# Second product of the first feed-forward in rounded high and low parts, with the square sums and first rows inside the last attention units

## The reference

```python
# layer 0
a = attention0(layernorm(x))        # 16 query heads, 4 key heads, head width 128, window 64 + first 32 keys
gu = ln @ ternary(w_gate_up).T      # 2048 columns: gate, up
h = silu(gate) * up                 # 1024 columns
hn = h / sqrt(mean(h * h) + eps)
f = hn @ ternary(w_proj).T          # 256 columns: the product this change touches
x = x + a_out * silu(f)             # a_out = attention output times wo0
# layer 1: the same frame, plain attention with 16 heads of width 16, feed-forward with gelu
x = x + a1_out * silu(gelu(ln @ W0.T + b0) @ W1.T + b1)
```

## Time and profile before

| | us |
|---|---|
| median of 3 runs | 816.56 (815.56 to 816.63) |
| the profiled execution's own time | 815.04 |
| its span | 813.2 |
| PE busy | 770.1 |
| DVE busy | 607.1 |
| ACT busy | 474.0 |
| POOL busy | 299.8 |

### The profile page before, as it was taken

The page is one execution under the profiler, slowest core; times in us unless marked ns, Lnnn a source line. Parts: engine busy times, 40 slices in busy tenths (PEclk is TensorE's granted clock), DMA queues, the critical chain, the costliest instruction groups (busy, mean ns, idle before and its releaser), DMA issues.

```text
span 813.2 us, 13362 instructions
## 1 busy us (share of the span) xinstructions
PE 770.1 (95%) x4656; PEld 475.5 (58%) x4656; DVE 607.1 (75%) x1632; ACT 474.0 (58%) x968; POOL 299.8 (37%) x255
## 2 busy tenths in 40 slices
PE   4977899899999999999999999999999999999996
PEld 2555578555356667846446667856436667865543
DVE  6979887679766766788857677887958677787852
ACT  3888872535867773243777675143795765233583
POOL 1358770401028882002008885002005887100201
PEclk9989999999999999999999999999999999999998
DMA  9311012381013110084003120047002200027300
GB/s 302 105 46 46 1 32 81 123 224 44 3 33 87 59 33 1 1 253 112 2 13 101 33 65 2 1 156 208 3 2 52 80 21 1 1 77 216 73 3 26
DMA packets 56818, 55.37 MB, mean 68 GB/s; under 512 B 14256, under 2 KB 43312, under 8 KB 56752
## 3 DMA queue, kind: packets, MB, share of 16 engines
q1 hardware_dynamic: 52768, 49.63, 21.5%
q10 hardware_dynamic: 3664, 3.84, 1.7%
q0 software_dynamic: 320, 1.05, 0.4%
HBM read 39.00 MB, written 15.24 MB: 67 GB/s over the span
## 4 chain that ended last, share of the span: by engine, by line
PE 68%; issue 12%; DVE 8%; ACT 5%; POOL 5%; DMA 1%; ACTq 0%; SPq 0%; POOLq 0%; DVEq 0%
PE bank L931 13%; PE bank L1042 7%; PE bank L1249 6%; PE bank L1233 5%; PE bank L966 5%; PE bank L1144 5%; PE bank L1028 5%; PE bank L1172 4%; PE bank L1216 3%; PE bank L1009 3%; PE bank L977 2%; PE bank L1221 2%; POOL region L598 2%; PE bank L991 2%; POOL region L602 2%
## 5 line engine op out<-in xcount | busy, mean ns | idle before, releaser
L1605 DVE TENSOR_REDUCE mx<-bank 128x1 f32<-128x512 f32 x256 | 161.2, 684 | 28.2 <-PE bank L1172 23.1
L602 POOL TENSOR_TENSOR region<-region 128x512 f32<-128x512 f32 x75 | 100.3, 1337 | 148.0 <-DVE region L1423 143.3
L931 PE MATMUL bank<-xnT,wrope 128*128 128x512 f32 x320 | 147.4, 604 | 5.2 <-DVE th L1446 2.1
L883 ACT ACTIVATE region<-bank 128x512 f32<-128x512 f32 x256 | 132.9, 602 | 25.5 <-PE bank L1221 24.2
L762 ACT ACTIVATE region<-region,nb 128x128 f32<-128x128 f32 x256 | 81.5, 390 | 57.1 <-DVE nb L1435 56.8
L931 PEld LDWEIGHTS bank<-xnT,wrope 128*128 128x128 f32 x320 | 58.9, 194 | 67.5 <-issue 62.9
L598 POOL TENSOR_TENSOR region<-region,sin_sb 128x512 f32<-128x512 f32 x60 | 81.5, 1358 | 40.7 <-ACT region L742 40.1
L631 POOL TENSOR_TENSOR region<-region,bo_bc 128x256 f32<-128x256 f32 x16 | 11.6, 727 | 204.6 <-DVE region L1484 204.6
L1416 DVE TENSOR_TENSOR region<-bank,cos_sb 128x512 f32<-128x512 f32 x80 | 54.3, 686 | 34.5 <-PE bank L931 34.2
L740 ACT ACTIVATE region<-bank 64x512 f32<-64x512 f32 x80 | 47.5, 594 | 48.7 <-DVE region L1416 39.2
L966 PE MATMUL bank<-region 128*128 128x128 f32 x512 | 73.1, 287 | 1.0 <-POOL region L602 1.0
(11 more groups left out here) (143 smaller groups left out, 1344.8 us busy)
## 6 DMA issues: line engine op xcount, KB each, us to landing
wrope<-in_wrope SPq DMA_DIRECT2D x80, 128.0 KB, 2.2
scratch<-region SPq DMA_DIRECT2D x16, 512.0 KB, 5.0
Qp<-scratch SPq DMA_DIRECT2D x56, 128.0 KB, 3.6
Kp<-scratch SPq DMA_DIRECT2D x56, 128.0 KB, 3.7
scratch<-region SPq DMA_DIRECT2D x16, 256.0 KB, 5.4
X<-in_x SPq DMA_DIRECT2D x4, 512.0 KB, 4.1
out<-X SPq DMA_DIRECT2D x16, 128.0 KB, 2.1
VW<-v_rows SPq DMA_DIRECT2D x16, 102.0 KB, 2.7
```

Source lines behind the costliest of these rows:

```text
L602: nc.gpsimd.tensor_tensor(dst, dst, tiles(sw[:, r % 2, :], i), ALU.add)\
L883: nc.scalar.activation(P1[:, n % 8, :], turned_bank(n)[:, :], ACT.Exp, scale=SCALE1)\
L931: mm = nc.tensor.matmul(misc(b, name)[:, 0:width], lhs(c), xnT[:, c, :], start=(c == 0), stop=(c == DC - 1))
L1605: nc.vector.tensor_reduce(mx1[:, g % 2, column:column + 1], scores_bank(m)[:, :], AX.X, ALU.max)\
```

## The change

The second product takes its weights from two rounded copies of `H` (`H_hi` and `H_lo`, which lie in the buffers `Qp` and `Kp`), and `wpT` is stored rounded as well. ACT writes `H_hi` (`high_rows`), DVE writes `H_lo = H - H_hi` (`low_rows1`). Each 8-chunk product of a tile becomes 16 products of rounded values. The sums of squares stand in unit 16 with a bank of their own, tile 0 behind them, tile 1 in unit 17. The root is scaled by one half (`4.0 / HID`), the tanh reads the product's bank with the root as its scale, the gate reads the bank too, and the residual is added with the root as its factor, so that L1539 is gone. `rsqrt` has 11 links. `FFN_LATER` is another list, and the raw pieces of the weights that lay in `wpT` lie in `H`.

```diff
-RSQRT = 13
+RSQRT = 11
@@ misc_jobs
-    jobs += [("proj", 0), ("proj", 1), ("ot", 1), ("wo0", 0), ("wo0", 1), ("proj", 2), ("proj", 3)]
-    jobs += [("xh", 0), ("wo0", 2), ("wo0", 3), ("xh", 1), ("v1", 0)] + ...
+    jobs += [("sum", 0), ("proj", 0), ("proj", 1), ("proj", 2), ("ot", 1), ("wo0", 0), ("wo0", 1), ("proj", 3)]
+    jobs += [("wo0", 2), ("wo0", 3), ("xh", 0), ("xh", 1), ("v1", 0)] + ...
-FFN_LATER = [0, 0, 2, 2, 0, 0, 2, 2, 0, 0, 2, 2, 2, 1, 1, 0]
+FFN_LATER = [0, 1, 1, 2, 0, 1, 2, 2, 0, 1, 2, 2, 1, 1, 0, 0]
+def ups_at(b, s):
+    return [i for kind, i in ffn_at(b, s) if kind == "up"] if 0 <= s < NKV * TT else []
-        wpT = sb("wpT", [P, HC, DIM])
+        wpT = sb("wpT", [P, HC, DIM], F32R)
+        H_hi, H_lo = Qp, Kp
-        wp_flat = wpT[:, :, :].rearrange("p c n -> p (c n)")
+        h_room = [h_flat[:, n * SEQ:n * SEQ + PIECE] for n in (HC - 3, HC - 5)]
@@ scalar
+            def high_rows(b, i):
+                act.wait_ge(h_ready.sem, h_ready.at(b, i + 1))
+                nc.scalar.activation(H_hi[:, i, :], H[:, i, :], ACT.Copy).then_inc(hhi_ready.sem, 1)
+                    for i in ups_at(b, s - 1):
+                        high_rows(b, i)
-                turned_outputs(b, 1)
                 for t in range(TT):
-                    act.wait_ge(f_ready.sem, f_ready.at(b, t + 1))
-                    nc.scalar.activation(TE0[:, t, :], F[:, t, :], ACT.Tanh, scale=0.5)\
+                    if t == 2:
+                        turned_outputs(b, 1)
+                    misc_wait(act, b, ("proj", t))
+                    if t == 0:
+                        act.wait_ge(fr_step.sem, fr_step.at(b, RSQRT))
+                    nc.scalar.activation(TE0[:, t, :], misc(b, ("proj", t))[:, 0:DIM], ACT.Tanh, scale=rstd[:, t:t + 1])\
@@ tensor
-                        mm = nc.tensor.matmul(misc(b, ("proj", t))[:, 0:DIM], H[:, c, t * P:(t + 1) * P],
-                                              wpT[:, c, :], start=(c == 0), stop=(c == HC - 1))
+                        if t == 0:
+                            pe.wait_ge(hlo_ready.sem, hlo_ready.at(b, c + 1))
+                        for part in (H_hi, H_lo):
+                            mm = nc.tensor.matmul(misc(b, ("proj", t))[:, 0:DIM], part[:, c, t * P:(t + 1) * P],
+                                                  wpT[:, c, :], start=(c == 0 and part is H_hi),
+                                                  stop=(c == HC - 1 and part is H_lo))
+                def square_sums():
+                    pe.wait_ge(sq_ready.sem, sq_ready.at(b, 1))
+                    misc_take(pe, b, ("sum", 0))
+                    pe.wait_ge(mx0_done.sem, mx0_done.at(b, NT * (NKV * TT - 1)))
+                    ...
                     if s == NKV * TT:
-                        pe.wait_ge(h_ready.sem, h_ready.at(b, HC))
-                        projected(0)
+                        square_sums()
+                    if s >= NKV * TT:
+                        misc_done(projected(s - NKV * TT), ("proj", s - NKV * TT))
-                misc_done(projected(1), ("proj", 1))
-                turn_outputs0(b, 1)
-                projected(2, 0, 2)
+                misc_done(projected(2), ("proj", 2))
+                turn_outputs0(b, 1)
+                projected(3, 0, HC // 2)
                 pe.wait_ge(ot_ready.sem, ot_ready.at(b, 2))
                 output0(0)
                 output0(1)
-                misc_done(projected(2, 2), ("proj", 2))
-                misc_done(projected(3), ("proj", 3))
-                turn_half(b, 0)
+                misc_done(projected(3, HC // 2), ("proj", 3))
                 output0(2)
                 output0(3)
+                turn_half(b, 0)
@@ vector
+            def gate0(b, t):
+                misc_wait(dve, b, ("proj", t))
+                gate_of(b, 0, t, misc(b, ("proj", t))[:, 0:DIM])
+            def low_rows1(b, i):
+                dve.wait_ge(hhi_ready.sem, hhi_ready.at(b, i + 1))
+                nc.vector.tensor_tensor(H_lo[:, i, :], H[:, i, :], H_hi[:, i, :], ALU.subtract)\
+                    .then_inc(hlo_ready.sem, 1)
+                    for i in ups_at(b, s - 2) if s >= NKV * TT else ():
+                        low_rows1(b, i)
+                    if s == NKV * TT:
+                        misc_wait(dve, b, ("sum", 0))
+                        rsqrt(misc(b, ("sum", 0))[:, 0:TT], 4.0 / HID, 16 * EPS_RMS, fr_step, b, 0)
                     ... (first_blocks, ternary steps, gate and times_up)
+                    for i in ups_at(b, s - 2) if s < NKV * TT else ():
+                        low_rows1(b, i)
+                    if s == NKV * TT + 1:
+                        gate0(b, 0)
-                    for t in pair:
-                        gated_ffn(t)
-                    for t in pair:
-                        gate_of(b, 0, t, F[:, t, :])
-                    for t in pair:
-                        gated_attention(t)
+                    if h == 0:
+                        gate0(b, 1)
+                        for t in pair:
+                            gated_attention(t)
+                        for t in pair:
+                            row_stats(b, 1, t)
+                    else:
+                        for t in pair:
+                            gate0(b, t)
+                            gated_attention(t)
+                            row_stats(b, 1, t)
```

More of the change, by code:

```diff
@@ L71, in misc_jobs @@
         jobs += [("wt", k) for k in TURN_AT.get(s, ())] if b == 0 else []
-    jobs += [("proj", 0), ("proj", 1), ("ot", 1), ("wo0", 0), ("wo0", 1), ("proj", 2), ("proj", 3)]
-    jobs += [("xh", 0), ("wo0", 2), ("wo0", 3), ("xh", 1), ("v1", 0)] + [("qk", j) for j in range(4)] + [("v1", 1)]
+    jobs += [("sum", 0), ("proj", 0), ("proj", 1), ("proj", 2), ("ot", 1), ("wo0", 0), ("wo0", 1), ("proj", 3)]
+    jobs += [("wo0", 2), ("wo0", 3), ("xh", 0), ("xh", 1), ("v1", 0)] + [("qk", j) for j in range(4)] + [("v1", 1)]
     jobs += [("dup", i) for i in range(HC)] + [("mt", 0)] + [("down", t) for t in range(TT)]
@@ L87, in misc_order @@
     return order
-PLACED = {"xt": (2, 6), "xh": (3, 0), "qk": (1, 2, 3, 4), "v1": (5, 7), "dup": (2, 2, 2, 2, 3, 4, 2, 3), "down": (4, 1, 2, 3), "mt": (2, 2, 3, 2)}
-LENT = {("rope", 1): 3, ("rope", 2): 4, ("wo1", 1): 3, ("wo1", 2): 4, ("wo1", 3): 5, ("proj", 2): 4, ("proj", 3): 5, ("wo0", 2): 0, ("wo0", 3): 6}
+PLACED = {"xt": (2, 6), "sum": (5,), "xh": (3, 0), "qk": (1, 2, 3, 4), "v1": (5, 7), "dup": (2, 2, 2, 2, 3, 4, 2, 3), "down": (4, 1, 2, 3), "mt": (2, 2, 3, 2)}
+LENT = {("rope", 1): 3, ("rope", 2): 4, ("wo1", 1): 3, ("wo1", 2): 4, ("wo1", 3): 5, ("proj", 2): 4, ("proj", 3): 5, ("wo0", 0): 3, ("wo0", 1): 6, ("wo0", 2): 0, ("wo0", 3): 6}
 def misc_banks(order):
@@ L402, in released @@
                 "up": lambda: [(h_ready, n + 1)],
-                "proj": lambda: [(f_ready, n + 1)],
+                "proj": lambda: [(g_ready, n + 1)],
+                "sum": lambda: [(fr_step, 2)],
                 "wo0": lambda: [(sg_step, n + 1)],
@@ L1041, in projected @@
                     for c in range(first, last):
-                        mm = nc.tensor.matmul(misc(b, ("proj", t))[:, 0:DIM], H[:, c, t * P:(t + 1) * P],
-                                              wpT[:, c, :], start=(c == 0), stop=(c == HC - 1))
-                    return mm
+                        if t == 0:
[4 more added lines that the diff above has]
+                                                  stop=(c == HC - 1 and part is H_lo))
+                    return mm
+                def square_sums():
+                    pe.wait_ge(sq_ready.sem, sq_ready.at(b, 1))
+                    misc_take(pe, b, ("sum", 0))
+                    pe.wait_ge(mx0_done.sem, mx0_done.at(b, NT * (NKV * TT - 1)))
+                    for n in range(TT):
+                        mm = nc.tensor.matmul(misc(b, ("sum", 0))[:, n:n + 1], sq[:, 1, n * P:(n + 1) * P],
+                                              ones1[:, :], start=True, stop=True)
+                    misc_done(mm, ("sum", 0))
                 for s in range(NKV * TT + 2):
                     if s == NKV * TT:
-                        pe.wait_ge(h_ready.sem, h_ready.at(b, HC))
-                        projected(0)
+                        square_sums()
+                    if s >= NKV * TT:
+                        misc_done(projected(s - NKV * TT), ("proj", s - NKV * TT))
                     if s < NKV * TT:
@@ L1067, in _ @@
                         turn_weights(k // 2, k % 2)
[L1070 to L1074, removed]
                 def output0(t):
@@ L1365, in rsqrt @@
                     lambda: nc.vector.scalar_tensor_tensor(out=y, in0=a, scalar=1.5, in1=y,
+                                                           op0=ALU.add, op1=ALU.mult),
+                    lambda: nc.vector.tensor_tensor(a, y, y, ALU.mult),
+                    lambda: nc.vector.tensor_tensor(a, a, h, ALU.mult),
+                    lambda: nc.vector.tensor_scalar(v, a, 1.5, 2.5, ALU.mult, ALU.add),
```

(14 more changed lines are left out.)

20 lines of the change are left out of this document (6 added, 14 removed).

## The result

The changed kernel takes **832.25 us** (median of 5 runs, 827.48 to 833.91); the kernel before took 816.22 beside it (5 runs, 815.28 to 816.63). The ratio is 1.0192 (95% interval 1.0159 to 1.0225): slower by 16.0 us. The forecast was 820.6, range 810 to 830: the direction was right, the loss was four times the one forecast (4.1), and the time lies above the range. The profiled execution took 827.48 us (span 825.6, mean granted clock 0.977). It is the shortest of the five; the other four took 831.53 to 833.91 at 0.970 to 0.975. The profiled execution of before took 815.04 (span 813.2, clock 0.989). So the two traces show 12.4 us of the loss, and the rest lies in executions without a trace.

The account below looks back on a forecast made before the run. PE was taken to bound units and tail of batches 1 to 3, with DVE counting in batch 0. First norm -0.4, batch 0 +5.7, batches 1 to 3 -1.2: +4.1 on 815.04, 819.1; median 1.5 above, 820.6 us, range 810 to 830.

Parts of the forecast that it names:

- PE's price: Second product on PE: a rounded 256-column product takes 0.13 us, a tile 2.08 for 3.56, 23.7 us less in all.
- Rival 3: Second product on PE: the rounded product is no faster, at 0.235 us each; +27.6, 844 us; chance 0.05.
- What is added: Per batch, eight copies on ACT at some 0.6 us and eight subtractions on DVE at 0.7 or 1.1 us.
- Rival 2: DVE and POOL block each other: at 1.5 us a subtraction, +11.6, 828 us; chance 0.12.
- Tail of batches 1 to 3: Sums at 316.4, then DVE is the path: `turn_half(1)` at 339.95 for 340.37; three batches -1.2 us.
- expected second gap: Tail of batch 1: PE, ready at 338.7, waits for DVE's normalised rows ahead of `turn_half(1)` at 339.95.
- Batch 0: Seven subtractions cost +5.0 in the units, PE waits for POOL's squares, the tail is 0.7 late: +5.7 us.
- Units of batches 1 to 3: DVE's subtractions make PE reach unit 16 at 316.4 instead of 313.8 in batch 1, 2.6 us late; bounds 0 and 4.
- Rival 1: Units of batches 1 to 3: subtractions fall into DVE's idle time and PE's gain survives; 809.7 us; chance 0.26.
- Rival 4: The terms cancel: units late by 1.5 instead of 2.6 us in three batches, -3.3, 817.3 us; chance 0.15.

Follow-up runs that it names:

- warm: The changed kernel with needless products on PE in its long waits, which nobody reads; 826.19 us, ratio 1.0124 to the kernel before.
- no_low: The changed kernel without DVE's subtractions, the product taking H_hi twice, so the low part is missing; 818.13 us, ratio 1.0032 to the kernel before.
- rsqrt11_before: The kernel before with 11 links in the root chain instead of 13, nothing else; 813.07 us, ratio 0.9973.
- few_squares_before: The kernel before, with POOL squaring only the last of the eight parts of H; 816.13 us, ratio 1.0006.

## Why the prediction was right in direction and wrong in size

**PE's price: right.** Timeline of PE in tile 0 of batch 1, the kernel after: products 0.12 us apart (forecast 0.13).

```profile
326.95 0.28 PE L1062 MATMUL bank<-wpT,Kp 128*128 128x256 f32 x1
327.07 0.28 PE L1062 MATMUL bank<-wpT,Qp 128*128 128x256 f32 x1
```

The rule of the Trainium skill that was weighed ("TensorE: Matmul & The Clock Gate", section "The mechanism": loads overlap only where row groups differ) fails here again: these products have a load of 0.20 us each (its group's mean is 197 ns) and start every 0.12. The same section also lets a load run ahead when it goes to a background weight buffer; the pace agrees with that, though no run here shows where a load goes. Rival 3 is dead. Tiles take 2.0 to 2.1 us at full clock, four a batch, so some 23.7 us were taken off PE's products. PE is busy only 10 us less, and most of the difference is the clock: layer 1's q and k products alone are busy 42.2 us for 33.2 (in warm 33.6).

**What is added: right.** Groups of the kernel after, busy us and mean ns of one:

```profile
L1522 DVE TENSOR_TENSOR Kp<-H,Qp 128x512 fp32r<-128x512 f32 x32 | 31.2, 976 | 0.0
L706 ACT ACTIVATE Qp<-H 128x512 fp32r<-128x512 f32 x32 | 19.9, 621 | 0.1
```

Copies 0.62 us (forecast 0.6); subtractions 0.68 at the least and 0.98 in the mean, for 0.7 and 1.1 at the two prices. Rival 2 wanted 1.5: single ones reach 1.78, the mean doesn't. Its 828 lies nearer to the measured time than the forecast does, but by another way.

**Tail of batches 1 to 3: right but for the clock.** Sums to `turn_half(1)`: 23.93, 25.25 and 23.98 us, forecast 23.55 (339.95 - 316.4). DVE is the path, and PE waits 2.35 us for the normalised rows ahead of `turn_half(0)`, as forecast (it was to be at 333.1 and is at 335.86, 2.7 later, as the sums are). The expected second gap, ahead of `turn_half(1)`, isn't there, though DVE's chain was not too dear: PE filled it with slow products. In warm, where they take 0.22 us each, the gap is back with 1.0 us, and sums to `turn_half(1)` is 23.49 in every batch: against that the low clock cost 0.4, 1.8 and 0.5 here.

**Batch 0: the units and the wait right, the total by luck.** +6.9 for +5.7. From unit 6 on PE comes 4.85 us later to the place of the sums (forecast 5.0) and waits 3.06 us there for POOL's last square and sum (forecast 3.6). But from the sums to `turn_half(1)` it takes 27.3 us, forecast 23.55: 3.75 more. In warm, where PE doesn't stand ahead of the sums, it is 23.49, so this is the low clock. That the total came out near is the 1.9 us that this trace gained ahead of unit 6. Timelines of POOL and PE, the kernel after:

```profile
123.04 1.42 POOL L620 TENSOR_TENSOR region<-H 128x512 f32<-128x512 f32 x1 [2.53 <-DVE H L1482]
124.53 2.13 POOL L623 TENSOR_TENSOR region<-region 128x512 f32<-128x512 f32 x1
```
```profile
126.71 0.59 PE L1072 MATMUL bank<-ones,region 128*128 128x1 f32 x2 [3.06 <-POOL region L623]
```

`turn_half(1)` is at 154.0, forecast 152. Not foreseen: the clock of 0.50 over the 4.8 us behind that wait, and again from 147 to 152, in the q and k products.

**Units of batches 1 to 3: the step that failed.** "It is 2.6 us late, for DVE" should have read 5.3 (4.4 in batches 2 and 3: sums 70.96 and 70.95 us behind the first scores, for 66.56). Of DVE's times worked out for batch 1, all are late by one constant (timeline of DVE, first masks of units 10, 12 and 14, and two subtractions, one with POOL at work and one without):

```profile
302.99 1.34 DVE L1522 TENSOR_TENSOR Kp<-H,Qp 128x512 fp32r<-128x512 f32 x1
...
305.68 0.28 DVE L1464 CUSTOM_DVE_ANT_0 region<-bank,mask_rest 128x128 f32<-128x128 f32 x1
...
314.23 0.68 DVE L1522 TENSOR_TENSOR Kp<-H,Qp 128x512 fp32r<-128x512 f32 x1
314.82 0.28 DVE L1464 CUSTOM_DVE_ANT_0 region<-bank,mask_first 128x128 f32<-128x128 f32 x1
...
322.24 0.28 DVE L1464 CUSTOM_DVE_ANT_0 region<-bank,mask_rest 128x128 f32<-128x128 f32 x1
```

Less 6.54 they are at 299.1, 308.3 and 315.7, forecast 297.4, 306.5 and 314.0: 1.7, 1.8 and 1.7 late. From unit 10 to unit 14 the working was exact to 0.1 us; the 1.7 us arose before it, where I had added up DVE's new instructions on the old times of PE. The same masks without the subtractions (no_low, its timeline of DVE):

```profile
301.92 0.28 DVE L1464 CUSTOM_DVE_ANT_0 region<-bank,mask_rest 128x128 f32<-128x128 f32 x1
...
310.46 0.28 DVE L1464 CUSTOM_DVE_ANT_0 region<-bank,mask_first 128x128 f32<-128x128 f32 x1
...
316.94 0.28 DVE L1464 CUSTOM_DVE_ANT_0 region<-bank,mask_rest 128x128 f32<-128x128 f32 x1
```

Less 4.20 (its batch 1 starts at 251.43) they are at 297.7, 306.3 and 312.7. So at unit 10 the new list by itself makes 2.9 us, and the sum had 1.5 for it (0.93 for one extra job and 0.6 for `up 4`). The new list puts ten jobs ahead of unit 10 where there were eight, and both extra ones hold up PE's scores of that unit. The subtractions make 1.4 there (the sum had 1.1), 2.0 at unit 12 and 3.0 at unit 14. And PE itself, which the sum let run without a wait, waited in unit 7 for a bank that ACT's swap of the rotary rows freed late. Timeline of PE, the kernel after:

```profile
287.65 0.73 PE L1045 MATMUL bank<-xnT_hi,wguT 128*128 128x512 f32 x2 [1.03 <-ACT region L754]
```

Without the subtractions this wait is 0.4 (no_low), in the kernel before there is none. How the 1.7 divides between this wait and the second job is not shown. The other 1.0 us of batch 1 arose at the end: PE waited 0.98 us for exps and 1.09 for `o_turned`, and then worked at a mean clock of 0.68: eight scores 1.38 us instead of 0.92 (L983; 0.115 each in the earlier trace rows), two groups of four transposes 0.85 each instead of 0.44 (L1019, L994; the next such group, at 328.91, takes 0.44 again). That is 1.3 us.

**The clock: in no step.** The working took every duration of PE from stretches at full clock, and found in three places that PE would wait 1 to 4 us, without asking what it does after that. In the trace of after the tails of the four batches lost 6.5 us by it (3.8, 0.4, 1.8 and 0.5 against 23.49), the runs 5.5 (warm).

The median missed by 11.65 us. The profiled execution, 827.48 for 819.1, missed by 8.4: the start 1.2, batch 0 1.2, the units of batches 1 to 3 6.3 (2.7, 1.8, 1.8), their tails 2.5 against the forecast's 23.55; 2.7 came back in layer 1, which the sum left out (1.6 of it in the last stage, which rsqrt11_before gains by its two links alone). The other 3.3 us are that the median lies 4.8 above the profiled execution and not 1.5. These executions have no trace; their lower clock (0.970 to 0.975 for 0.977) points at stretches like that between 50 and 55 us.

**The rivals.** Rival 1 named a marker, unit 14's first mask at 311.5 or 314.0: it came at 315.7, and PE's gain is not seen. Rival 4 (late by 1.5) falls with it. None had the clock, and none asked what the order is worth without the product. The chance of 0.59 for slower was well placed; the range of 8 in 10 ended 2.25 us too low.

## What to carry to other kernels

Work moved from a full engine to one that idles 30% of the time isn't free when that engine feeds the full one in turn: here 8 subtractions of 1 us cost 2.5 to 3.8 us between first scores and sums in every batch (no_low), about half of the 6 that the shorter products gave. When a forecast has the engine of the products wait a microsecond or more, price what runs behind that wait at the lower clock too, and ask whether anything needless could fill it. Before a trace of one execution is set beside another, compare a stretch that the change leaves alone: here such a stretch of batch 0 differed by 1.9 us. And time each part of a bundled change alone, in both orders: here the one that pays is the smallest, two links fewer.

## What the runs showed of the hardware

The clock can fall behind waits of PE of 1 to 3 us, and doesn't always. After 3.06 us the window 126.7 to 131.5 was granted 0.50, with rounded products of 256 columns 0.21 us apart instead of 0.12, and full pace again at 131.5; after 2.35 and 0.69 us of waits, 0.50 again in 343.7 to 346. Behind two waits of about 1 us the mean was 0.68 in 321 to 325.6. In batch 0 PE waits 1.8 and 1.3 us ahead of 49 us in the traces of before and of few_squares_before alike; then the clock between 50 and 55 us is 0.54 in the one and 1.00 in the other, and unit 6 starts 1.9 us apart. So the kernel before has such stretches too, and one trace doesn't tell how often.

The Trainium skill says it in "TensorE: Matmul & The Clock Gate", section "What's actually happening": the array is throttled by default and activity releases it; the trace agrees on the two levels, 0.50 and 1.00. What surprised was the size: some 5.5 us of 832 between kernels whose PE work differs only in products that nobody reads, and a spread of 6.4 us in five runs of one kernel (827.48 to 833.91), where the kernel before spreads 1.4 in five and up to 3.2 in thirteen.
